# Turning half of the probability tiles of a cross-attention kernel with a DMA transpose, and computing scores eight units ahead

## The reference, cut to what matters

```python
scores_t = jnp.einsum('bhsd,bhtd->bhst', q, k_t) * attn_scale
probs_t = jax.nn.softmax(scores_t, axis=-1)
text_out = jnp.einsum('bhst,bhtd->bhsd', probs_t, v_t)
...
attn_scores = jnp.einsum('bhsd,bhnd->bhsn', q, k_ip) * attn_scale
qsem = jnp.einsum('bhst,bte->bhse', probs_t, text_ehs)
qsem = _l2norm(qsem)
ip_n = _l2norm(ip_ehs)
sem = jnp.einsum('bhse,bne->bhsn', qsem, ip_n)
...
fused = attn_scores + SEM_SCALE * sem
probs_ip = jax.nn.softmax(fused, axis=-1)
probs_ip = probs_ip * spatial_mask[None, None, :, None]
ip_out = jnp.einsum('bhsn,bhnd->bhsd', probs_ip, v_ip)
...
out = text_out + IP_SCALE * ip_out
out = out @ W_out + b_out
out = out + residual
```

## Time and profile before

| | |
|---|---|
| time, median of three runs | 1905.04 us (1903.60 to 1912.46) |
| profiled execution, time | 1911.86 us |
| profiled execution, span | 1910.1 us |
| TensorE busy in the span | 1878.8 us |
| VectorE, ScalarE, GpSimd busy | 1460.1, 1378.5, 907.3 us |

### The profile page before, as it was taken

How to read it: one execution, slowest core, us unless ns; L and a number is a source line. 1 busy time by engine, 2 the same in 40 slices (tenths; PEclk the granted TensorE clock), 3 DMA queues, 4 the chain that set the end, 5 groups by cost and what they waited for, 6 DMA issues and landing times.

```text
span 1910.1 us, 52608 instructions
## 1 busy us (share of the span) xinstructions
PE 1878.8 (98%) x15701; PEld 1275.4 (67%) x15701; DVE 1460.1 (76%) x3192; ACT 1378.5 (72%) x2644; POOL 907.3 (47%) x1076
## 2 busy tenths in 40 slices
PE   5999999999999999999999999999999999999999
PEld 3776667666666666666666666666666666666555
DVE  5454544788888888888888888888888888888885
ACT  3344554788888888888888888888888888888611
POOL 2121222455555555555555555555555555555421
PEclk8899999999999999999999999999999999999999
DMA  5345555111111111111111111111111111111023
GB/s 174 105 133 130 165 141 140 40 26 27 45 26 27 27 43 26 27 41 29 26 27 45 26 27 27 43 26 27 27 43 27 27 26 44 28 27 51 1 86 107
DMA packets 120643, 102.10 MB, mean 53 GB/s; under 512 B 53369, under 2 KB 114433, under 8 KB 120609
## 3 DMA queue, kind: packets, MB, share of 16 engines
q1 hardware_dynamic: 118304, 99.50, 19.3%
q10 hardware_dynamic: 2304, 2.14, 0.4%
HBM read 67.21 MB, written 34.39 MB: 53 GB/s over the span
## 4 chain that ended last, share of the span: by engine, by line
PE 96%; DVE 2%; ACT 1%; issue 0%; DMA 0%; SPq 0%; ACTq 0%; DVEq 0%
PE bank L1291 29%; PE bank L1292 18%; PE bank L1272 15%; PE bank L1157 13%; PE bank L1265 7%; PE bank L1297 3%; PE bank L1358 3%; PE bank L1290 3%; PE bank L1216 1%; PE bank L1359 1%; DVE reduced L894 1%; DMA reduced<-in_ctx 0%; PE bank L1343 0%; PE bank L1140 0%; ACT u_sb L688 0%
## 5 line engine op out<-in xcount | busy, mean ns | idle before, releaser
L509 POOL TENSOR_TENSOR weight<-probs,half_hi 128x508 f32<-128x508 f32 x640 | 736.1, 1150 | 649.4 <-DVE discard L973 640.1
L1291 PE MATMUL bank<-u_sb,probs_hi 127*128 127x508 f16 x2560 | 943.4, 375 | 0.0
L1292 PE MATMUL bank<-u_sb,probs_hi 127*128 127x508 f16 (+3 forms) x2560 | 760.8, 297 | 0.0
L966 DVE TENSOR_REDUCE neg_max<-bank 128x1 f32<-128x508 f32 x640 | 439.4, 687 | 239.1 <-PE bank L1265 239.1
L712 ACT ACTIVATE probs_hi<-bank 127x512 f16<-127x512 f32 x640 | 382.1, 597 | 234.8 <-PE bank L1272 234.8
L1290 PE MATMUL bank<-v_ring,probs_hi 127*128 127x41 f16 x2560 | 468.5, 183 | 0.0
L978 DVE SCALAR_TENSOR_TENSOR probs_lo<-bank,probs_hi 127x512 f16<-127x512 f32 x640 | 438.8, 686 | 2.4 <-ACT probs_hi L712 2.4
L701 ACT ACTIVATE probs<-bank,neg_max 128x508 f32<-128x508 f32 x640 | 434.3, 679 | 0.5 <-DVE neg_max L966 0.4
L973 DVE SCALAR_TENSOR_TENSOR discard<-bank,weight 128x508 f32<-128x508 f32 x640 | 433.4, 677 | 1.1 <-PE bank L1292 1.1
L708 ACT ACTIVATE half_hi<-probs 128x508 f16<-128x508 f32 x640 | 401.4, 627 | 20.4
L1290 PEld LDWEIGHTS bank<-v_ring,probs_hi 127*128 127x128 f16 x2560 | 248.0, 97 | 226.2 <-issue 0.8
(11 more groups left out here) (160 smaller groups left out, 1340.1 us busy)
## 6 DMA issues: line engine op xcount, KB each, us to landing
x_sb<-in_x SPq DMA_DIRECT2D x16, 640.0 KB, 5.4
reduced<-in_ctx SPq DMA_DIRECT2D x32, 256.0 KB, 5.1
q_ring<-q_parts SPq DMA_DIRECT2D x160, 48.0 KB
k_ring<-k_parts SPq DMA_DIRECT2D x160, 47.6 KB
u_parts<-u_sb SPq DMA_DIRECT2D x8, 825.5 KB, 4.2
u_sb<-u_parts SPq DMA_DIRECT2D x8, 825.5 KB, 4.7
v_parts<-v_sb SPq DMA_DIRECT2D x8, 820.0 KB, 8.0
v_ring<-v_parts SPq DMA_DIRECT2D x160, 41.0 KB
```

The costliest lines, as they stand in the source:

```text
L509: nc.gpsimd.tensor_tensor(weight[:, st % 2, :], probs[:, st, :], half_hi[:, st % 2, :], ALU.subtract)\
L966: nc.vector.tensor_reduce(neg_max[:, st:st + 1], bank[S_BANK + st % 2][:, 0:T], AX.X, ALU.max, negate=True)\
L1291: nc.tensor.matmul(y, hi_k, u_sb[0:TP, par, GH[k]:GH[k] + T], start=(k == 0), stop=False)
L1292: last = nc.tensor.matmul(y[:, k * TP:T], hi_k, u_sb[0:TP, par, UL[k]:UL[k] + U_COLS[k]], start=False, stop=(k == TT - 1))
```

## The change

Units are handled in pairs. The even ones keep the TensorE transposes. For the odd ones, the exponential gets a larger bias (`shift`, so that the values come out scaled), ScalarE copies them to fp16 in the layout of the query rows (`flat_hi`), GpSimd makes the remainder (`remainder`), and a DMA on SP's queue transposes both halves at once, a tile of 128 x 1024 fp16, into `turned` (`turn`). GpSimd forms the factor of the norm of an odd unit as the `probs` tile plus the remainder (`weigh_odd`), in place; even units have a subtraction as before (`weigh_even`). VectorE's `lo` and ScalarE's `hi` and `halve` are left for even units alone.

The scores are issued eight units ahead in place of two (`LEAD`), the transposes three (`T_LEAD`), and `probs` is a ring of ten. The two score banks stay two: the scores of unit j wait for the exponential of unit j - 2. A round is 40 units, written out, and there are 16; before, a block was 16 units. SP loads five heads by seven DMAs, twice in a round, into one of two groups of buffers, between its transposes; all of it starts once the last batch of phase 1 has been stored, since `q_ring`, `k_ring`, `turned` and `flat` now lie over tiles of phase 1. Both Gram matrices of the first two batches are loaded then, and the first quad waits for both.

The columns of W_q, W_k and W_k_ip are put in another order before the launch (d before h), so that five heads are one run in HBM. For this GpSimd builds a second mask, `spreadmask`, in 16 steps that each wait for the one before, counted in `CONSTS`; and the twelve matmuls of the image scores have 80 columns in place of 32 or 16.

The core of the diff:

```diff
+    GROUP = 5
+    ROUND = 2 * GROUP * ST
+    ROUNDS = UNITS // ROUND
+    LEAD, T_LEAD = 8, 3
+    PROB_RING, RING = 10, 4
+    PAIRS_PER_ROUND = ROUND // 2
...
+    q_parts = nc.dram_tensor("q_parts", [B, 3, D, H, S], bf16).ap()
+    k_parts = nc.dram_tensor("k_parts", [B, 3, D, H, T], bf16).ap()
...
+        probs = sb("probs", [P, PROB_RING, T], fp32)
+        neg_max = sb("neg_max", [P, 4], fp32)
+        exp_bias = sb("exp_bias", [P, 4], fp32)
...
+        t_end = RING * 2 * TT * P
+        turned = late16[:, 0:t_end].rearrange("p (r a k s) -> p r a k s", r=RING, a=2, k=TT)
...
+        half_hi = late16[:, t_end + 4 * S:t_end + 4 * S + RING * T].rearrange("p (r t) -> p r t", r=RING)
+        flat = wkv[:, 0:RING * 2 * TT * P].rearrange("p (r a k t) -> p r a k t", r=RING, a=2, k=TT)
+        q_ring = work[0:KS, 0:2 * GROUP * S // 2].bitcast(bf16).rearrange("p (n h s) -> p n h s", n=2, h=GROUP)
+        k_ring = x_sb[0:KS, :, :, :].rearrange("p r s c -> p (r s c)")[:, 0:2 * GROUP * T // 2].bitcast(bf16)\
+            .rearrange("p (n h t) -> p n h t", n=2, h=GROUP)
...
+        def load_group(eng, b, i, n):
+
+            heads = bass.ds(i * GROUP, GROUP)
+            for a0, copies in ((0, 3), (3, 2), (5, 1)):
+                eng.dma_start(q_ring[a0 * D:(a0 + copies) * D, n], q_parts[b, 0:copies, :, heads, :].rearrange("a d h s -> (a d) h s"))\
+                   .then_inc(group_loaded[n], 16)
+            for part, (a0, copies) in enumerate(((0, 3), (3, 2), (5, 1))):
+                eng.dma_start(k_ring[a0 * D:(a0 + copies) * D, n],
+                              k_parts[b, part, :, heads, :].unsqueeze(0).broadcast_to([copies, D, GROUP, T]))\
+                   .then_inc(group_loaded[n], 16)
...
+        def load_values(eng, b, i, n):
+            eng.dma_start(v_ring[:, n].rearrange("p h k c -> p h (k c)"),
+                          v_parts[b, bass.ds(i * GROUP, GROUP), :, :].rearrange("h p c -> p h c")).then_inc(values_loaded[n], 16)
...
-            with sp.Fori(1, B // 2) as pair:
+            sp.wait_ge(bank_filled[IPS_JOB[0]], use(IPS_JOB, B - 1))
+            for n in range(2):
+                load_group(sp, 0, n, n)
+                load_values(sp, 0, n, n)
+            for par in range(2):
+                sp.dma_start(u_sb[:, par, :], u_parts[par]).then_inc(u_loaded, 16)
+            sp.wait_ge(flat_padded, 1)
+
...
+            def turn(rnd, j):
+
+                sp.wait_ge(flat_lo_ready, nth(rnd, j) + 1)
+                apart(sp)
+                need(sp, unit_done, ROUND * rnd + j + 1 - 2 * RING)
+                apart(sp)
+                r = j // 2 % RING
+                sp.dma_start_transpose(turned[:, r].rearrange("p a k s -> p (a k) s"),
+                                       flat[:, r].rearrange("p a k t -> p (a k t)")).then_inc(turned_landed[r], 16)
+
+            LOAD_AT = 9
+
+            def turns(rnd, b, half, u_par, first, last):
+                for j in range(1, ROUND, 2):
+                    turn(rnd, j)
+                    n = j // (ROUND // 2)
+                    if j % (ROUND // 2) == LOAD_AT and not (first and n == 0) and not (last and n == 1):
+
+                        free = 1 - n
+                        sp.wait_ge(scores_filled, ROUND * rnd + n * ROUND // 2)
+                        apart(sp)
+                        sp.wait_ge(unit_done, ROUND * rnd + n * ROUND // 2)
+                        apart(sp)
+                        nb, i = (b, half * 2 + 1) if n == 0 else (b, 2) if half == 0 else (b + 1, 0)
+                        load_group(sp, nb, i, free)
+                        load_values(sp, nb, i, free)
+                    if j == 15 and half == 0 and u_par is not None:
+
+                        sp.wait_ge(quad_filled, ROUND * rnd)
+                        apart(sp)
+                        sp.dma_start(u_sb[:, u_par, :], u_parts[b + 1]).then_inc(u_loaded, 16)
+
+            turns(0, 0, 0, None, True, False)
+            turns(1, 0, 1, None, False, False)
+            with sp.Fori(0, B // 2 - 1) as pair:
                 for par in range(2):
-
...
+            for d in range(D):
+                if d:
+                    pool.wait_ge(consts_made, 14 + d)
+                nc.gpsimd.affine_select(out=spreadmask[:, :, :], in_=spreadmask[:, :, :], compare_op=ALU.not_equal, fill=1.0,
+                                        base=-H * d, pattern=[[P, NC], [-1, H]], channel_multiplier=1).then_inc(consts_made, 1)
...
+            def remainder(rnd, j):
+
+                pool.wait_ge(flat_hi_ready, nth(rnd, j) + 1)
+                rows = flat_rows(j)
+                nc.gpsimd.tensor_tensor(rows[:, 1, :, 0:TP], probs[:, j % PROB_RING, :].rearrange("p (k t) -> p k t", k=TT),
+                                        rows[:, 0, :, 0:TP], ALU.subtract).then_inc(flat_lo_ready, 1)
+
+            def weigh_odd(rnd, j):
+
+                pool.wait_ge(flat_lo_ready, nth(rnd, j) + 1)
+                own = probs[:, at(rnd, j)[1] % PROB_RING, :].rearrange("p (k t) -> p k t", k=TT)
+                nc.gpsimd.tensor_tensor(own, own, flat_rows(at(rnd, j)[1])[:, 1, :, 0:TP], ALU.add).then_inc(odd_weight_ready, 1)
+
+            def weigh_even(rnd, j):
+
+                pool.wait_ge(half_ready, nth(rnd, j) + 1)
+                pool.wait_ge(probs_t_filled, nth(rnd, j) + 1)
+                own = probs[:, at(rnd, j)[1] % PROB_RING, :]
+                nc.gpsimd.tensor_tensor(own, own, half_hi[:, at(rnd, j)[1] // 2 % RING, :], ALU.subtract).then_inc(even_weight_ready, 1)
 
...
+            REDUCE_AT = LEAD + 1 + ST - 1
+
+            def units(rnd, first):
+                for j in range(ROUND):
+                    if j % 2 == 1:
+                        remainder(rnd, j)
+                        if not (first and j < 2):
+                            weigh_odd(rnd, j - 2)
+                    elif not (first and j < 6):
+                        weigh_even(rnd, j - 6)
+                    if j % ST == REDUCE_AT % ST and not (first and j < REDUCE_AT):
+                        reduce_head(ROUND // ST * rnd + (j - REDUCE_AT) // ST, (j - REDUCE_AT) // ST % 2)
...
+            act.wait_ge(parts_saved, 1 + 16 * 2 * NC * B)
+            act.wait_ge(v_saved, 1 + 16 * B)
+            act.wait_ge(u_saved, 1 + 16 * B)
...
+            def shift(rnd, j):
+
+                rnd, j = at(rnd, j)
+                act.wait_ge(row_max_found, ROUND * rnd + j + 1)
+                nc.scalar.activation(exp_bias[:, j % 4:j % 4 + 1], neg_max[:, j % 4:j % 4 + 1], ACT.Copy, bias=LOG_SCALE)\
+                  .then_inc(bias_ready, 1)
...
+            def exp(rnd, j):
+
+                if j % 2 == 1:
+                    act.wait_ge(bias_ready, nth(rnd, j) + 1)
+                else:
+                    act.wait_ge(row_max_found, ROUND * rnd + j + 1)
+                need(act, norms_done, ROUND * rnd + j + 1 - PROB_RING)
+                bias = exp_bias if j % 2 == 1 else neg_max
+                nc.scalar.activation(probs[:, j % PROB_RING, :], bank[S_BANK + j % 2][:, 0:T], ACT.Exp,
+                                     bias=bias[:, j % 4:j % 4 + 1]).then_inc(probs_ready, 1)
...
+            def flat_hi(rnd, j, first):
+
+                act.wait_ge(probs_ready, ROUND * rnd + j + 1)
+                if not (first and j < 2 * RING):
+                    landed(act, rnd, j - 2 * RING)
+                    need(act, odd_weight_ready, nth(rnd, j) + 1 - RING)
+                nc.scalar.activation(flat_rows(j)[:, 0, :, 0:TP], probs[:, j % PROB_RING, :].rearrange("p (k t) -> p k t", k=TT),
+                                     ACT.Copy).then_inc(flat_hi_ready, 1)
...
+            def hi(rnd, j):
+
+                act.wait_ge(probs_t_filled, nth(rnd, j) + 1)
+                rnd, j = at(rnd, j)
+                need(act, unit_done, ROUND * rnd + j - 3)
+                r = j // 2 % 2
+                nc.scalar.activation(probs_hi[:, r, :], bank[PT_BANK + r][0:TP, 0:S], ACT.Copy, scale=PROB_SCALE)\
                   .then_inc(hi_ready, 1)
...
+            def units(rnd, first):
+
+                for j in range(ROUND):
+                    if j % 2 == 1 and not (first and j < HI_AT):
+                        hi(rnd, j - HI_AT)
+                    exp(rnd, j)
+                    if j % 2 == 0:
+                        shift(rnd, j + 1)
+                        halve(rnd, j)
+                    else:
+                        flat_hi(rnd, j, first)
+                    if j % 2 == (DRAIN_AT + 1) % 2 and not (first and j < DRAIN_AT + 1):
+                        g, st = (j - DRAIN_AT) // ST, (j - DRAIN_AT) % ST
+                        drain_out(ROUND // ST * rnd + g, st // 2, g % 2)
...
+            def row_maximum(rnd, j):
+                dve.wait_ge(scores_filled, ROUND * rnd + j + 1)
+                need(dve, probs_ready, ROUND * rnd + j - 3)
+                nc.vector.tensor_reduce(neg_max[:, j % 4:j % 4 + 1], bank[S_BANK + j % 2][:, 0:T], AX.X, ALU.max, negate=True)\
```

(61 more changed lines are left out.)

309 lines of the change are left out of this document (121 added, 188 removed).

## The result

The changed kernel takes 1829.74 us (median of four runs, 1824.02 to 1836.30), the kernel before 1907.99 us (median of four, 1903.60 to 1912.46). The ratio is 0.9591, 95% interval 0.9546 to 0.9636: 4.1% faster. The profiled execution took 1832.93 us with a span of 1831.2, against 1911.86 and 1910.1 before: 78.9 us less. The forecast was 1790 us, with a range of 1768 to 1880.

A forecast was written before the change was run, and what follows sets the result against it. TensorE was taken to bound the kernel: 1911.9 - 140.8 (odd transposes) + 4.8 (start) + 3.0 (image scores) + 20.8 (passage) - 2.6 = 1797.1 us, against the median 1790.3; predicted 1790, range 1768 to 1880.

The forecast's parts named there:

- The pair of 4.08 us: Main loop: two units cost TensorE 2 x (1.60 + 0.22) + 0.44 = 4.08 us once odd units' transposes leave it.
- rival A: Loop: TensorE stays the bound, 1770 to 1825 us; chance 0.62 together with the case of a costlier passage.
- B: Loop: ScalarE or GpSimd sets the pair, back edges counted for it; examples 1851 and 1892 us; chance 0.23.
- The prediction's own signs: Changed profile: quads 4.08 us apart over two units, no TensorE idle in mid-loop, GpSimd about 91% busy.
- C: Loop: DMA transposes outlast their pair, TensorE waits in `landed`, kernel slower, up to 4200 us; chance 0.15.
- The DMA transpose: SP's queue, odd units: one turn taken as 2.9 us, inside the pair of 4.08.
- No cost is seen at the back edge now: Loops written out by 40 units: no cost in the sum; if code were fetched again, 16 times a few us.
- must land by slot 12, 17 us later: Group loads in the loop: issued after unit 9's turn, some 3 us into slot 3; taken as hidden.
- The passage: From last Gram store to first quad: waits for loads and scores ahead, +20.8 us, bounds 12 and 28.
- The start: Before the first work: the mask's 16 dependent steps at 0.3 us each, +4.8 us.
- Phase 1: Image scores with 80 columns: +3 us over 8 batches, with 10 kept in the range.
- the forecast's own term for the scores that are no longer there: Loop: eight scores and two transposes issued during the passage leave the loop, -2.6 us.

## Why the prediction was right in its mechanism and 40 us low

*The pair of 4.08 us* was right to the hundredth, and with it the mechanism of rival A. The time of 1829.74 lies above A's own 1770 to 1825 all the same: it is in the part of the range that was there for B. In the profiled pair the misses add up to 48 us (1.3 at the start, 9.5 in the passage, 37.1 in the loop), and 12.1 came back in phase 1 by a clock that nobody had forecast. Part of the closeness is luck.

The prediction's own signs were mixed. TensorE did wait in the loop, 8.0 us of it for turned tiles, which was named as the sign of C. C's mechanism, a turn that takes longer than its pair, wasn't there: 1.4 us of all engines a turn. The sums of the others hold: GpSimd's three operations are 1.12, 1.12 and 1.15 us and half a reduction 0.28, 3.67 a pair against 3.72 forecast. Rival B as an engine's bound is out; the back edges, which it also named, came.

*The DMA transpose*: bounds 1.5 to 11.6 us, taken 2.9, measured 1.4 to 1.5. The lower end, in proportion to bytes, was the right one. The upper end rested on pieces of 64 bytes, for which no row spoke; a turn's packets are 256 bytes each (5120 of them in the 5.0 turns above). In mid-loop C was nowhere near. A lone turn lands in 3.1 us. The Trainium skill's 1309 ns for 128 x 128, from *VectorE: DVE Perf Modes*, is a time for one small transpose; eight blocks at once took 1.4 to 1.5 us of the engines together, SP being held for 1.23. So it is not to be multiplied by blocks.

*"No cost is seen at the back edge now"* is the step that failed, 17.6 us. A body of 40 units, written out, is not the body of 16 for which nothing was seen: the code of TensorE is fetched again at some of its back edges, as the prediction had put it behind an "if". The price named beside it, "16 times a few us", was put into rival B and not into the sum. There are eight back edges and not 16; it came at four, with 2.8 to 3.1 us of wait, and behind three of them 1.3 to 1.6 more at the lower clock.

*The group loads*: "must land by slot 12, 17 us later" looked at the loads' own due time. What was late was the turn behind them, held up by k's three loads: 13.3 us.

*The passage*: +20.8 forecast, +30.3 measured, beyond the upper bound of 28. Store to first load 3.7 us (4.5 forecast); first load to first scores 13.8 us (6.3 forecast), again the loads of k: splitting them alone brought this to 6.9 us, and store to first quad from 34.3 down to 22.8; the scores ahead, at the pace of ScalarE, 12.3 us where nothing else was waited for (354.28 to 366.55 in the run with the first Gram tile alone; 14 forecast); and 4.3 us of wait for the Gram tiles.

*The start*: the 16 steps take 0.38 us each, not 0.3: +6.1 against +4.8.

*Phase 1*: the image scores cost +0.37 a batch, the 3 us of the forecast. That the clock mostly stays up behind them was not seen: -12 us in the profiled pair; what it is in the medians no trace shows. By medians the whole change is -78.3, by the profiled executions -78.9, so the difference between the two kinds of sum is small here.

*The end of the loop*: not in the sum, 6.3 us. The last five pairs took 3.7 us more than 4.08 each; in the two kernels with ScalarE's order changed they took 2.6 less, which is the forecast's own term for the scores that are no longer there. ScalarE drains before it makes `hi`, TensorE waits twice for 2.2 us, and the lower clock follows.

Open: what decides at which back edges of the inner loop TensorE's code is fetched again (two in the changed kernel, none to three in others with the same loops), and how often the clock falls in phase 1 in a run without a profile.

## What to carry to other kernels

When a bound engine is relieved, write down for each queue what stands directly ahead of the new transfers: a broadcast written as outermost dimension made three loads slow and every transfer behind them late, and taking it out gave 26 us in 1830, of which some 20 can be traced to the loads. A lead is cover for the orders of all engines, not only for the transfer that it was made for; before shortening it, look up whose turn stands behind the early product. Price an unrolled loop body at its back edges even if the shorter one shows nothing there, and look at the packets of the instruction queue at the place; add to each wait of TensorE what it then loses at the lower clock.

## What was not expected of the hardware

- A DMA transpose of 128 x 1024 fp16 from SBUF to SBUF takes 1.4 to 1.5 us of the 16 engines, lands in 3.1 us and holds SP for 1.23 us; two in 4.08 us ran beside TensorE with no loss.
- Loads with 3 and 2 repeated copies outermost delayed what stood behind them: v landed in 9.0 us against 3.6, the longest turn in 11.4 against 4.9. Of k's packets 3.7 were under way at a time, of q's, of the same size and number, 13.
- A back edge of a written-out body of 40 units cost TensorE 2.3 to 3.8 us of wait at two to five of its eight passes, with nine more 16 KB packets of code for each, and none where the loop was written out altogether.
- After a wait of 2.8 to 4.5 us TensorE's granted clock read 0.65 and 0.50 on average over the next 4 us, in part or wholly the 1.2 GHz level. Gram matmuls behind 24 fp32 matmuls with 32 or 16 columns took 4.31 us (granted clock 0.60), behind 24 with 80 columns 2.63 (1.00) most times.
